# Another order of products and readers in attention units that carry expert work, and turns by true transposes

## What is computed

```
xn = layernorm(x)
q, k, v = heads(xn @ Wq + bq), heads(xn @ Wk + bk), heads(xn @ Wv + bv)      # 16 heads of 8
attn = softmax(q @ k.T / sqrt(8)) @ v
a = merge(attn) @ Wo + bo
topk_vals, topk_idx = top_k(xn @ router_w.T, 2)
g = sigmoid(topk_vals); g = g / (g.sum() + 1e-10)
for e in range(8):
    h = silu(xn @ w_gate[e]) * (xn @ w_up[e])
    out = out + ge[:, None] * (h @ w_down[e])                                # ge: the token's g for expert e, or 0
x + a + out
```

## Time and profile before

| | before |
|---|---|
| median of 3 runs | 907.96 us (907.85 to 909.28) |
| the profiled execution | 908.43 us |
| its span, first to last instruction | 906.7 us |
| TensorE matmul busy | 858.5 us (95%) |
| VectorE busy | 749.1 us (83%) |
| ScalarE busy | 692.8 us (76%) |
| GpSimd busy | 479.7 us (53%) |
| mean granted clock of TensorE | 0.977 |

### The profile page before, as it was taken

How to read it: one execution, slowest core, us unless ns; L and a number is a source line. 1 busy time by engine, 2 the same in 40 slices (tenths; PEclk the granted TensorE clock), 3 DMA queues, 4 the chain that set the end, 5 groups by cost and what they waited for, 6 DMA issues and landing times.

```text
span 906.7 us, 20365 instructions
## 1 busy us (share of the span) xinstructions
PE 858.5 (95%) x6773; PEld 488.6 (54%) x6773; DVE 749.1 (83%) x1381; ACT 692.8 (76%) x1525; POOL 479.7 (53%) x678
## 2 busy tenths in 40 slices
PE   8987766899999999999999999999999999999997
PEld 6744222245555565556556565555555565555542
DVE  6489999978888878888888878888888878888844
ACT  3543545668888888888888888888888888888896
POOL 8141053025666656666666656666666656666530
PEclk9998688999999999999999999999999999999999
DMA  5875050112433333233243333333323333332216
GB/s 159 188 231 184 2 122 25 31 40 62 96 83 84 83 78 77 65 79 74 71 95 84 84 83 78 79 71 81 75 64 91 83 82 86 80 87 54 52 17 186
DMA packets 86200, 78.04 MB, mean 86 GB/s; under 512 B 11416, under 2 KB 75680, under 8 KB 86064
## 3 DMA queue, kind: packets, MB, share of 16 engines
q1 hardware_dynamic: 72416, 66.49, 26.8%
q0 software_dynamic: 12672, 9.59, 8.2%
q10 hardware_dynamic: 1008, 0.66, 0.3%
HBM read 56.65 MB, written 21.69 MB: 86 GB/s over the span
## 4 chain that ended last, share of the span: by engine, by line
PE 86%; DVE 12%; ACT 1%; issue 1%; DMA 0%; ACTq 0%; DVEq 0%
PE ps L1081 27%; PE ps L1096 26%; PE ps L1071 9%; PE ps L1138 8%; DVE maxima L875 6%; PE ps L1126 4%; PE ps L1131 3%; PE ps L1109 2%; PE ps L982 1%; DVE xnT L857 1%; PE ps L1154 1%; PE ps L1103 1%; PE ps L987 1%; DVE stage L848 1%; PE ps L993 1%
## 5 line engine op out<-in xcount | busy, mean ns | idle before, releaser
L875 DVE TENSOR_REDUCE maxima<-ps 128x1 f32<-128x512 f32 x1024 | 639.7, 682 | 100.4 <-PE ps L1081 93.2
L589 ACT ACTIVATE probs<-ps 128x512 f32<-128x512 f32 x1024 | 540.3, 602 | 142.8 <-PE ps L1071 127.2
L1081 PE MATMUL ps<-qk 64*128 64x512 f32 x1024 | 421.0, 475 | 34.6 <-DVE maxima L875 33.7
L1071 PE MATMUL ps<-qk 64*128 64x512 f32 x1024 | 380.2, 456 | 0.0
L1081 PEld LDWEIGHTS ps<-qk 64*128 64x128 f32 x1024 | 187.4, 188 | 225.2 <-DVE maxima L875 182.9
L1096 PE MATMUL ps<-probs,v_all 128*9 128x512 f32 x2048 | 271.5, 603 | 1.7 <-ACT o_sb L595 1.1
L484 POOL DMA_INDIRECT acc<-result,idx x72 | 119.3, 1657 | 134.2 <-issue 125.6
L1138 PE MATMUL ps<-xg_T,gu_w 64*128 64x128 f32 x1152 | 189.0, 284 | 0.4
L1071 PEld LDWEIGHTS ps<-qk 64*128 64x128 f32 x1024 | 173.2, 186 | 10.0 <-ACT probs L589 8.0
L1138 PEld LDWEIGHTS ps<-xg_T,gu_w 64*128 64x128 f32 x1152 | 159.7, 186 | 22.7 <-PE ps L1138 2.8
L447 POOL DMA_INDIRECT xg<-rows,idx x72 | 72.9, 1012 | 55.9 <-issue 42.8
(11 more groups left out here) (150 smaller groups left out, 615.0 us busy)
## 6 DMA issues: line engine op xcount, KB each, us to landing
gu_w<-L_ffn_w_gate SPq DMA_DIRECT2D x72, 128.0 KB
gu_w<-L_ffn_w_up SPq DMA_DIRECT2D x72, 128.0 KB
dn_w<-L_ffn_w_down SPq DMA_DIRECT2D x72, 128.0 KB
qk<-q_parts SPq DMA_DIRECT2D x126, 64.0 KB
qk<-k_parts SPq DMA_DIRECT2D x126, 64.0 KB
k_parts<-stage SPq DMA_DIRECT2D x23, 256.0 KB, 3.3
q_parts<-stage SPq DMA_DIRECT2D x16, 256.0 KB, 3.5
rows<-x_sb SPq DMA_DIRECT2D x1, 2112.0 KB, 10.4
```

The costliest lines, as they stand in the source:

```text
L589: act.activation(probs[:, u % NPB, q, h, :], ps[:, BANK_OF[job], :], ACT.Exp).then_inc(s_read, 1)
L875: dve.tensor_reduce(maxima[:, p % 2, qt, h, k:k + 1], ps[:, x_bank(i), :], AX.X, ALU.max, negate=True).then_inc(x_read, 1)
L1071: pe.matmul(ps[:, bank, :], t[r, 1, kt * P:(kt + 1) * P], t[r, 0, q * CH:(q + 1) * CH], start=True, stop=True).then_inc(s_filled, 1)
L1081: pe.matmul(ps[:, bank, :], t[r, 0, qt * P:(qt + 1) * P], t[r, 1, k * CH:(k + 1) * CH], start=True, stop=True).then_inc(x_filled, 1)
```

## The change

Units with expert work get two new orders, ROWS_DOWN for "rows" and HIDDEN for "gate" and "up". In both, piece (0, 0) is the first product of the unit. In ROWS_DOWN piece (0, 1) comes before any product of the lower half, in HIDDEN one score stands between. ScalarE takes the expert work behind the third score (rows) or behind the second (gate and up) and no longer at the end of the unit (PIECE_BEHIND). Waits that named a certain score now name the last or first of the unit, whichever it is, by four small helpers. The turn of the gathered rows is issued with `is_transpose=True`.

```diff
--- before.py
+++ after.py
@@ -50,8 +50,11 @@
 
 
 PLAIN = (("max", 0, 0), ("score", 1, 0), ("max", 0, 1), ("score", 1, 1), ("max", 1, 0), ("score", 0, 0), ("max", 1, 1), ("score", 0, 1))
-MIXED = (("max", 0, 0), ("score", 1, 0), ("piece", 0, 0), ("score", 1, 1), ("piece", 0, 1), ("max", 1, 0),
-         ("max", 0, 1), ("piece", 1, 0), ("score", 0, 0), ("piece", 1, 1), ("score", 0, 1), ("max", 1, 1))
+HIDDEN = (("piece", 0, 0), ("score", 1, 0), ("max", 1, 0), ("score", 0, 0), ("piece", 0, 1), ("score", 1, 1), ("max", 0, 0),
+          ("max", 0, 1), ("piece", 1, 0), ("score", 0, 1), ("piece", 1, 1), ("max", 1, 1))
+ROWS_DOWN = (("piece", 0, 0), ("score", 1, 0), ("max", 1, 0), ("piece", 0, 1), ("max", 0, 0), ("max", 1, 1), ("score", 0, 0),
+             ("piece", 1, 0), ("score", 0, 1), ("piece", 1, 1), ("max", 0, 1), ("score", 1, 1))
+PIECE_BEHIND = {"rows": 3, "gate": 2, "up": 2}
 ALONE = (("max", 0, 0), ("max", 1, 0), ("max", 0, 1), ("max", 1, 1))
 LAST = (("score", 1, 0), ("score", 0, 0), ("score", 1, 1), ("score", 0, 1))
 
@@ -85,7 +88,10 @@
 
 def items_of(u):
 
-    items = MIXED if u in EXPERT_AT else LAST if u >= LAST_S else ALONE if u < 0 else PLAIN
+    if u in EXPERT_AT:
+        items = ROWS_DOWN if EXPERT_AT[u][0] == "rows" else HIDDEN
+    else:
+        items = LAST if u >= LAST_S else ALONE if u < 0 else PLAIN
     return [i for i in items if not (i[0] == "score" and not 0 <= u < U) and not (i[0] == "max" and u >= LAST_S)]
 
 
@@ -100,20 +106,22 @@
     for job in (("turn", 0), ("turn", 1), ("q", 0), ("k", 0), ("v", 0), ("q", 1), ("k", 1), ("v", 1)):
         plain(job)
     for u in UNITS:
+        taken = 0
         for n, (kind, a, b) in enumerate(items_of(u)):
             for job in CHUNK_AT.get((u, n), ()):
                 if job[0] != "lg":
                     plain(job)
             if kind == "score":
                 plain(("score", u, a, b))
+                taken += 1
+                if u in EXPERT_AT and taken == PIECE_BEHIND[EXPERT_AT[u][0]]:
+                    read.append(EXPERT_AT[u])
             if kind == "max":
                 x_no["max", u + LX, a, b] = len(x_no)
             if kind == "piece" and (a, b) == (0, 0):
                 opened.append(EXPERT_AT[u])
             if kind == "piece" and (a, b) == (1, 1):
                 filled.append(EXPERT_AT[u])
-        if u in EXPERT_AT:
-            read.append(EXPERT_AT[u])
         if u in MT_AT:
             plain(("shift", MT_AT[u]))
         if u in OT_AT:
@@ -271,6 +279,15 @@
         def s_taken(*job):
             return READ_NO[job] + 1
 
+        def scores_filled(u):
+            return max(s_full("score", u, h, q) for h in range(2) for q in range(2))
+
+        def scores_taken(u):
+            return max(s_taken("score", u, h, q) for h in range(2) for q in range(2))
+
+        def first_of(kind, u):
+            return next(i for i in items_of(u) if i[0] == kind)[1:]
+
         def x_full(*job):
             return X_NO[job] + 1
 
@@ -304,7 +321,7 @@
             def load_pair(p):
                 s, b, h0 = p % NQ, p // PPB, 2 * (p % PPB)
                 if p >= NQ:
-                    sp.wait_ge(s_filled, s_full("score", KT * (p - NQ) + KT - 1, 0, 1))
+                    sp.wait_ge(s_filled, scores_filled(KT * (p - NQ) + KT - 1))
                 for c in range(2 * b, 2 * b + 2):
                     sp.wait_ge(parts_stored[c], 80)
                 t = slice(b * S, (b + 1) * S)
@@ -433,7 +450,7 @@
                 number_tiles(k)
 
             def clear_shift(p):
-                pool.wait_ge(s_filled, s_full("score", KT * (p - NQ) + KT - 1, 0, 1))
+                pool.wait_ge(s_filled, scores_filled(KT * (p - NQ) + KT - 1))
                 for h in range(2):
                     pool.memset(qk[p % NQ][64 * h + 32:64 * h + 36, 0, :].bitcast(F32), 0.0).then_inc(pads_ready, 1)
                     pool.wait_ge(pads_ready, 4 * NQ + 2 * (p - NQ) + h + 1)
@@ -656,13 +673,15 @@
             for u in UNITS:
                 if u == RANKS_AT:
                     gate_exp()
+                taken = 0
                 for n, (kind, h, q) in enumerate(items_of(u)):
                     for job in CHUNK_AT.get((u, n), ()):
                         take_chunk_job(*job)
                     if kind == "score":
                         weights(u, h, q)
-                if u in EXPERT_AT:
-                    take_expert(*EXPERT_AT[u])
+                        taken += 1
+                        if u in EXPERT_AT and taken == PIECE_BEHIND[EXPERT_AT[u][0]]:
+                            take_expert(*EXPERT_AT[u])
                 if u == LOGITS_AT:
                     act.wait_ge(lg_ps, NC)
                     act.activation(lg[:, :, :].rearrange("p n e -> p (n e)"), ps[:, 7, 0:NT * NE], ACT.Copy).then_inc(lg_ready, 1)
@@ -1065,7 +1084,7 @@
             def score(u, h, q):
                 p, kt = u // KT, u % KT
                 t, r = qk[p % NQ], slice(64 * h, 64 * h + ROWS)
-                if kt == 0 and (h, q) == (1, 0):
+                if kt == 0 and (h, q) == first_of("score", u):
                     pe.wait_ge(m_in[p % 2], 32 * (p // 2 + 1))
                 bank = s_room("score", u, h, q)
                 pe.matmul(ps[:, bank, :], t[r, 1, kt * P:(kt + 1) * P], t[r, 0, q * CH:(q + 1) * CH],
@@ -1074,7 +1093,7 @@
             def find_max(x, h, k):
                 p, qt = x // KT, x % KT
                 t, r = qk[p % NQ], slice(64 * h, 64 * h + ROWS)
-                if qt == 0 and h == 0 and k == 0:
+                if qt == 0 and (h, k) == first_of("max", x - LX):
                     pe.wait_ge(qk_in[p % NQ], LOADS * (p // NQ + 1))
                     pe.wait_ge(pads_ready, 4 * NQ + 2 * max(p - NQ + 1, 0))
                 bank = x_room(X_NO["max", x, h, k])
@@ -1083,7 +1102,7 @@
 
             def weigh(v):
                 p, kt = v // KT, v % KT
-                pe.wait_ge(s_read, s_taken("score", v, 0, 1))
+                pe.wait_ge(s_read, scores_taken(v))
                 if kt == 0:
                     if p == 0:
                         pe.wait_ge(pv_zero, 1)
@@ -1129,7 +1148,7 @@
                         if h == 0:
                             pe.wait_ge(xg_in[c % 4], 16 * (c // 4 + 1))
                         mm = pe.matmul(ps[:, bank, 64 * h:64 * h + 64], xg[r, c % 4, 0:E], ident[r, r],
-                                       start=(h == 0 and c < 2), stop=(h == 1))
+                                       start=(h == 0 and c < 2), stop=(h == 1), is_transpose=True)
                 else:
                     s, a = c % 2, ("gate", "up").index(job)
                     if (h, part) == (0, 0):
```

## The result

| | before | after |
|---|---|---|
| median, runs of both on one chip | 907.9 us (6 runs) | 914.25 us (6 runs) |
| ratio after to before, 95% interval | | 1.0064 (1.005 to 1.0079) |
| the same in a second series | 909.0 us (11 runs) | 915.02 us (6 runs), 1.0058 (1.0039 to 1.0077) |
| the profiled execution, its span | 908.43, 906.7 us | 916.09, 914.3 us |
| units 28 to 244 in two profiles each | 678.0 and 677.1 us | 682.5 and 682.7 us |

The account below looks back on a forecast made before the run. TensorE was taken to bound, each unit being one chain of its products and waits. Terms -22.4 + 0.6 + 10.8 + 5.8 + 3.1 + 0.7 = -1.4 us on 908.43 gave 907.0, as median 906.6 us; range 896 to 919.

Parts of the forecast that it names:

- the late m10: Gate and up units: maximum (1, 0) reduced later, so m11, maximum (1, 1), waits until 1.52 us; 144 x 0.075 = +10.8 us.
- at the head: Gate units' first piece waits for ScalarE's `result` from the rows unit; 72 x 0.08 = +5.8 us.
- at o_sb: Once in eight units ScalarE takes `o_sb`, delaying the next unit's scores and last maximum; +3.1 us in all.
- +0.7 for split_max: Gate and up units: split_max's three short ops delay the next reductions 0.64 us, of which 0.1 reaches m11; +0.7 us.
- -22.4: 70 rows units with both works before and after: unit 2.92 us against 3.24, 70 x -0.32 us.
- +0.6: Four rows units without one of the works (0, 1, 72, 73) now meet the same wait; +0.6 us.
- Rival 1: Waits at the unit's head and at m11 smaller than charged: 901, 896 or, without both, 890 us; chance 0.27.
- Rival 2: ScalarE becomes the loop in gate and up units, two scores behind the piece: +14.4 us, 921; chance 0.15.
- Rival 3: Row-tiled transposes hold both halves of the array, on the chain of 72 units: +14.4 us, 921; chance 0.08.
- 4: Rival: the transpose flag doesn't make one record of two, so the turns do nothing: 907 to 911 us; chance 0.05.

Follow-up runs that it names:

- Experiment 4: Changed kernel, but in rows units ScalarE takes the expert work behind the second score, not the third: 908.61 us, ratio 0.9997 to the kernel before.
- 7: Changed kernel, but in units with expert work the reduction of maximum (1, 0) reads 256 of 512 columns: 902.93 us, ratio 0.9928 to the kernel before.
- 8: Changed kernel with the maximum (1, 0) reduction cut to 256 columns and, in HIDDEN, piece (1, 1) ahead of score (0, 1): 893.48 us, ratio 0.9818.
- 5: Changed kernel, but GpSimd's three operations that make hid treat 16 of 256 columns: 909.4 us, ratio 1.0002 to the kernel before.
- 6: Changed kernel, but split_max runs behind the first reduction of the next unit, not ahead of it: 907.88 us, ratio 0.9986 to the kernel before.
- 1: Kernel before with one edit, the turn of the gathered rows as a true transpose: 894.83 us, ratio 0.984 to the kernel before.

## Why the prediction was wrong

The time was held by the range, the sign was not. By its own steps, over the units 28 to 244 of the two first profiles:

- Gate units: charged 72 x 0.075 for the late m10, 5.8 at the head and 0.5 at o_sb, together 11.7 us. Measured 11.8. Experiment 4 shows the head wait by itself, 7 and 8 the other.
- Up units: charged 5.4 and 2.6 at o_sb, together 8.0, and with the gate units +0.7 for split_max. Measured 7.9; up 1 of the first profile of before was at 3.08, and against the second profile it is 8.7.
- Rows units: charged -22.4 and +0.6, and nothing for split_max. Measured -15.2. The rows units with nothing special about them are exactly at 2.92. **This is the step that failed**, and in one term: "The three short ops of split_max put the next reductions 0.64 us later", of which the prediction let 0.1 reach m11 "in gate and up units: +0.7". In gate and up units that holds (up 5 at 3.03, for the usual 2.92). In rows units the next reductions came another 0.70 later than that: the operation of L903 took 0.70 us for 0.17 (0.53 more) and that of L905 0.35 for 0.18 (0.17 more), since the two stood still while GpSimd worked. As split_max delays the first reduction, and that one releases the last maximum of the unit, TensorE pays it in full: in the unit shown the load of that maximum stands at 454.86, 2.32 after the unit's start and not 1.52. That is 8 x 0.70 = 5.6 us. Experiments 5 and 6 take it away by two ways, and rows 5 falls to 3.11 and 2.93. With it the sum of the prediction is -1.4 + 5.6 = +4.2, and the profiles say +4.5 to +5.6.
- Small misses in both directions: rows 3 by 0.08 and gate 0 by 0.1, together 1.6 us too little charged, gate 3 and gate 6 by 0.08 each too much. No experiment looks at them. The medians of the runs differ by 6.0 and 6.3 us, so about 1 us isn't placed.
- The reason for the miss was in the trace of before: the earlier trace rows are from an up unit, where the ops are free. In rows units of the same place L888 takes 0.67 us beside L470, and these units were at 3.36 and not 3.24. The group of L888 has a mean of 325 ns against 216 of its sister L884, on equal shapes. I took the price from one instance, and of GpSimd I asked whether its queue keeps its order, not what it does to VectorE. The collision depends on phases: from the start of attention, split_max comes at 1.35 us and not at 1.18, and GpSimd's product on gu at 1.28 and not at 1.51. Before, it met the last of the three operations; now it starts ahead of the first.
- Rival 1, smaller waits: refuted by the lengths of gate and up units, and by 4, 7 and 8. Rival 2, ScalarE as the loop: not in the usual units, all at 2.92; it shows only behind o_sb, as charged (up 2: 3.21). Rival 3 and 4: refuted by 1. None of the rivals was the one that happened. That the time lies in the range is no merit of the mechanism: the range was wide for rivals that didn't occur.

## What to carry to other kernels

Look at the spread of one short operation over places, not at its mean or at one instance: where a copy of it takes three times as long beside another engine's work, its time is a matter of phase, and any reordering draws anew. An instruction moved to the head of a unit exposes each wait that its neighbours used to cover; ask of every reader that comes late whether the first instruction waits for it. And test the parts of a change alone: here one flag is worth 14.7 us in the old order, and the new order of gate and up units with its reader costs 21 in the changed kernel.

## What the runs showed of the hardware

GpSimd's work can stop VectorE's. A 128x16 operation of VectorE with two inputs from SBUF goes from 0.17 to 0.70 us beside GpSimd's 128x256 product and ends 0.03 behind it. The Trainium skill has this on its page "SBUF — State Buffer", section "Who interferes with whom": a VectorE instruction with two SBUF inputs contends with a GpSimd instruction that reads SBUF. The trace agrees, and the reductions, which read PSUM, keep their 0.68. The one-input operation on line 905 is also held: 0.35 us for 0.18 beside L488, 0.68 to 0.74 beside L492 in experiment 6, and 0.72 beside a memset in experiment 4, where the two-input operation ahead of it (L903) keeps its 0.18 beside the same memset. An operation of VectorE that started first wasn't held: in all nine rows units behind split_max of the kernel after, L907 starts 0.01 us ahead of GpSimd's L492 and keeps its 0.19, while L492 takes 0.75 to 0.77 us for 0.73.

A float32 transpose of 64 rows in one half of the array takes one record where the product with the identity takes two, its load lasts 140 ns instead of 188, and it runs beside the other half's products. The Trainium skill's page "TensorEngine Tiling (Array Packing)", section Restrictions, rules the transposing mode out beside column tiling and names no such rule for row tiling; experiment 1 shows that it works and gains with row tiling.
